# Value products of two units in one block, and square roots moved behind the last split, in a decoder's grouped attention

## What is computed

```
q = (x @ wq.T).reshape(B, N, N_Q, HD).transpose(0, 2, 1, 3)
k = (x @ wk.T).reshape(B, N, N_KV, HD).transpose(0, 2, 1, 3)
v = (x @ wv.T).reshape(B, N, N_KV, HD).transpose(0, 2, 1, 3)
s = jnp.einsum('bhgnd,bhmd->bhgnm', qg, k) * scale
s = jnp.where(mask[None, None, None], s, jnp.asarray(-jnp.inf, s.dtype))
p = jax.nn.softmax(s, axis=-1)
o = jnp.einsum('bhgnm,bhmd->bhgnd', p, v)
return o.reshape(...) @ wo.T
...
x = _layernorm(x + _L1_attn_ref(x, L1_attn_wq, L1_attn_wk, L1_attn_wv, L1_attn_wo), axis=-1)
```

## Time and profile before

| | |
|---|---|
| Median of 3 runs | 1655.85 us (1654.79 to 1658.16) |
| The profiled execution | 1656.58 us, its span 1654.7 us |
| TensorE busy | 1582.0 us, 96% |
| VectorE, ScalarE, GpSimd busy | 59%, 40%, 11% |
| DMA | 75.18 MB, mean 45 GB/s |
| Sublayer D on the trace | from about 835 to 1418 us |
| Sublayer B on the trace | from about 182 to 783 us |

### The profile page before, as it was taken

The page is one execution under the profiler, slowest core; times in us unless marked ns, Lnnn a source line. Parts: engine busy times, 40 slices in busy tenths (PEclk is TensorE's granted clock), DMA queues, the critical chain, the costliest instruction groups (busy, mean ns, idle before and its releaser), DMA issues. The chain is left out here.

```text
span 1654.7 us, 22796 instructions
## 1 busy us (share of the span) xinstructions
PE 1582.0 (96%) x8512; PEld 1270.0 (77%) x8512; DVE 970.2 (59%) x1958; ACT 665.4 (40%) x1218; POOL 178.4 (11%) x134
## 2 busy tenths in 40 slices
PE   7999899999999999998989999999999999889998
PEld 6776777887787778776877788788878877777876
DVE  5998677757765775767424533452553346256655
ACT  4784443434433443434233323332332323346541
POOL 8101400000000000000240000000000000613330
PEclk9999999999999999999999999999999999999999
DMA  5110111101100110100111100110110100202221
GB/s 217 53 40 27 65 36 42 52 1 52 62 16 27 51 44 8 52 26 2 45 53 51 52 26 26 49 52 0 51 63 13 38 14 26 79 10 85 79 83 51
DMA packets 25883, 75.18 MB, mean 45 GB/s; under 512 B 3874, under 2 KB 4610, under 8 KB 25540
## 3 DMA queue, kind: packets, MB, share of 16 engines
q1 hardware_dynamic: 25412, 72.90, 13.1%
q0 software_dynamic: 384, 1.05, 0.2%
HBM read 71.84 MB, written 2.10 MB: 45 GB/s over the span
## 5 line engine op out<-in xcount | busy, mean ns | idle before, releaser
L83 PE MATMUL bankY<-sb_Dwo,sb_DoT 128*128 128x512 f32 x768 | 193.9, 402 | 0.3 <-DVE sb_DoT L1121 0.3
L83 PE MATMUL bankY<-sb_Bwo,sb_BoT 128*128 128x512 f32 x768 | 193.6, 401 | 0.2 <-DVE sb_BoT L1121 0.2
L83 PE MATMUL bankA<-sb_xT,sb_Bwq 128*128 128x512 f32 x768 | 191.6, 399 | 0.0
L83 PE MATMUL bankA<-sb_xT,sb_Dwq 128*128 128x512 f32 x768 | 189.9, 396 | 0.0
L83 PEld LDWEIGHTS bankY<-sb_Dwo,sb_DoT 128*128 128x128 f32 x768 | 141.0, 189 | 42.2 <-issue 13.3
L83 PEld LDWEIGHTS bankY<-sb_Bwo,sb_BoT 128*128 128x128 f32 x768 | 141.0, 189 | 41.9 <-issue 12.9
L83 PEld LDWEIGHTS bankA<-sb_xT,sb_Bwq 128*128 128x128 f32 x768 | 143.4, 190 | 34.3 <-issue 2.7
L83 PEld LDWEIGHTS bankA<-sb_xT,sb_Dwq 128*128 128x128 f32 x768 | 142.2, 188 | 33.9 <-issue 2.7
L1052 DVE TENSOR_TENSOR sb_BqT<-bankA,sb_Btable 128x512 f32<-128x512 f32 x64 | 44.3, 692 | 153.0 <-ACT sb_Bsw L949 153.0
L1088 DVE TENSOR_TENSOR sb_xtok<-sb_xtok,bankY 128x512 f32<-128x512 f32 x128 | 87.1, 681 | 54.6 <-PE bankY L83 54.5
L949 ACT ACTIVATE sb_Bsw<-bankA 64x512 f32<-64x512 f32 x160 | 94.8, 593 | 54.8 <-PE bankA L83 51.6
(11 more groups left out here) (286 smaller groups left out, 2917.8 us busy)
## 6 DMA issues: line engine op xcount, KB each, us to landing
sb_raw<-in_w_attn SPq DMA_DIRECT2D x80, 512.0 KB, 3.4
sb_raw<-in_q_gu SPq DMA_DIRECT2D x22, 256.0 KB, 2.7
sb_raw<-in_q_d SPq DMA_DIRECT2D x11, 256.0 KB, 2.6
sb_raw<-in_wqk SPq DMA_DIRECT2D x8, 256.0 KB, 2.6
sb_rawx<-in_xT SPq DMA_DIRECT2D x4, 512.0 KB, 6.8
sb_raw<-in_ctxT SPq DMA_DIRECT2D x4, 512.0 KB, 6.0
sb_xtok<-in_x_tok SPq DMA_DIRECT2D x1, 2048.0 KB, 12.7
sb_raw<-in_ctx_tok SPq DMA_DIRECT2D x4, 512.0 KB, 3.8
```

The source lines that it names most:

```text
L83: last = nc.tensor.matmul(out, lhs, rhs, start=start and i == 0, stop=stop and i == len(pairs) - 1)
```

## The change

In D (without `rope`) the value products of units u-1 and u are made together in the odd turn u, unit by unit into two halves of `bankO`; one copy and one split of twice the width serve both. Y stands two units behind: turn u makes Y(u-2), between S(u+2) and the value products, and turns 7 and 15 end with Y(u-1), Y(u). From unit 10 of the last pass value products, copies and splits are single again. The exponential of u+2 stands ahead of the copy of `bankO` on ScalarE. Residual adds are three units behind. In B the value products stay single and in their places, though in two halves of `bankO` by turns, and Y stays one behind. In both, the first group's square roots stand behind the copy of unit 15, and the residual add of unit 13 with its statistics stands behind the split of unit 15.

```diff
-            oT = [[sb(mem, f"{tag}oT{i}{p}", [P, GROUP, 2, S], F32R) for p in range(2)] for i in range(2)]
+            oT = [sb(mem, f"{tag}oT{p}", [P, 2, GROUP, 2, S], F32R) for p in range(2)]
...
+            behind = 2 if rope else 3
...
+            def alone(u, final):
+                return rope or (final and u >= 10)
+            def attended(u, last):
+                return (u,) if alone(u, last) else (u - 1, u) if u % 2 else ()
...
+                    def attend(part, u):
+                        units = attended(u, part.final)
+                        if units and u < NT:
+                            pe.wait_ge(v_done, part.it * 4 + u // 2 + 1)
+                        for v in units:
+                            if v == units[0]:
+                                pe.wait_ge(pt_done, part.unit(u) + 3)
+                                pe.wait_ge(o_low, part.unit(v) + 1)
+                            for b in range(2):
+                                rows = slice(S * b, S * b + S)
+                                done = nc.tensor.matmul(bankO[:, b, side(v)], V[rows, v % NT, v // NT * HD:(v // NT + 1) * HD], pt[v % 2][rows, :], start=True, stop=True)
+                            done.then_inc(o_ready, 1)
...
-                            if late(u):
+                            if rope and late(u):
                                 output(part, u - 1)
...
+                            elif not rope and u % NT >= 2:
+                                output(part, u - 2)
+                            attend(part, u)
+                            if rope and u % NT and not late(u):
                                 output(part, u - 1)
...
                             if u % NT == NT - 1:
+                                if not rope:
+                                    output(part, u - 1)
                                 output(part, u)
...
+                            if not rope and not late(u) and (u + 2 < SLOTS or not part.final):
                                 exp(part, u + 2)
+                            units = attended(u, part.final)
+                            if units:
+                                act.wait_ge(o_ready, part.unit(u) + 1)
+                            if len(units) == 1:
+                                nc.scalar.activation(of_unit(0, u), unit_bank(u), ACT.Copy).then_inc(o_high, 1)
+                            elif units:
+                                nc.scalar.activation(of_pair(0), pair_bank, ACT.Copy).then_inc(o_high, 2)
...
+                            if part.final and u == SLOTS - 1:
+                                ln_roots(act, norm + 1, 0)
...
-                            if part.final and u == SLOTS - 2:
-                                ln_roots(act, norm + 1, 0)
...
-                            if u % NT >= 2:
-                                residual(part, u - 2)
+                            if u % NT >= behind and not (rope and part.final and u == SLOTS - 1):
+                                residual(part, u - behind)
...
                             if u % NT == NT - 1:
+                                if not rope or part.final and u == SLOTS - 1:
+                                    residual(part, u - 2)
                                 residual(part, u - 1)
```

More of the change, by code:

```diff
@@ L873, in output @@
                         pe.wait_ge(y_done, part.unit(u) + 1)
-                        pairs = [x for h in range(GROUP) for x in three([o[:, h].rearrange("p b q -> p (b q)") for o in oT[u % 2]], [w[:, h, :] for w in wo])]
+                        pairs = [x for h in range(GROUP) for x in three([o[:, u % 2, h].rearrange("p b q -> p (b q)") for o in oT], [w[:, h, :] for w in wo])]
                         if u % NT == NT - 1:
@@ L900, in turn @@
                                 project(part, banks[0])
-                            if late(u):
+                            if rope and late(u):
                                 output(part, u - 1)
-                            if u < NT and u % 2 == 0:
-                                pe.wait_ge(v_done, part.it * 4 + u // 2 + 1)
-                            pe.wait_ge(pt_done, part.unit(u) + 3)
-                            pe.wait_ge(o_low, part.unit(u) + 1)
-                            for b in range(2):
-                                rows = slice(S * b, S * b + S)
-                                done = nc.tensor.matmul(bankO[:, b, 0:GROUP * S], V[rows, u % NT, u // NT * HD:(u // NT + 1) * HD], pt[u % 2][rows, :], start=True, stop=True)
-                            done.then_inc(o_ready, 1)
-                            if u % NT and not late(u):
+                            elif not rope and u % NT >= 2:
+                                output(part, u - 2)
+                            attend(part, u)
+                            if rope and u % NT and not late(u):
                                 output(part, u - 1)
@@ L1004, in turn @@
                                 queries_or_keys(part, banks[0])
[L1005 to L1008 removed]
+                            if not rope and not late(u) and (u + 2 < SLOTS or not part.final):
                                 exp(part, u + 2)
+                            units = attended(u, part.final)
[5 more added lines that the diff above has]
+                                nc.scalar.activation(of_pair(0), pair_bank, ACT.Copy).then_inc(o_high, 2)
+                            if rope and not late(u) and (u + 2 < SLOTS or not part.final):
+                                exp(part, u + 2)
+                            if part.final and u == SLOTS - 1:
+                                ln_roots(act, norm + 1, 0)
                             if u in VALUES_AT and not part.final:
```

22 lines of the change are left out of this document (15 added, 7 removed).

## The result

| | before | with the change |
|---|---|---|
| first set, median (least to most) | 1656.21 us (1654.79 to 1658.16), 4 runs | 1644.95 us (1642.64 to 1646.71), 4 runs |
| ratio, 95% interval | | 0.9929 [0.9917, 0.9941] |
| second set, median | 1658.81 us, 17 runs | 1642.99 us (1642.41 to 1646.24), 6 runs |
| ratio, 95% interval | | 0.9911 [0.9895, 0.9928] |
| profiled execution: its time, its span | 1656.58, 1654.7 us | 1642.64, 1640.7 us |

The kernel became faster by 0.7 to 0.9%. The forecast was 1640.3 us and its range 1636.5 to 1646.5: the time lies inside, 4.65 us above the forecast in the first set and 2.7 in the second. Against the kernel before of the same set it is 11.3 and 15.8 us less, where the sum said 15.5. The profiled execution, against which the sum was made, came 14.0 us lower.

What follows compares the result with a forecast made beforehand. TensorE, busy 96% of the span, was taken to bound the kernel. 11.9 - 2.1 + 3.3 + 2.4 = 15.5 us off 1655.85 gave 1640.3 us; range 1636.5 to 1646.5.

Steps and rivals of the forecast that it cites:

- Value products by twos: D's loop: two value products in one block cost 1.25 us instead of 1.66; 0.41 saved in 29 pairs, 11.9 us.
- The rival from the Trainium skill: D's pairs: the second unit's weight loads aren't hidden, or a pair drains in part; 6.4 us less gain, 1647; 6%.
- Waits in D's loop: D, turns 1 and 9: TensorE waits 0.25 us for the wider split ahead of Y(0) and Y(8); eight places, -2.1 us.
- The end of D: A(15)'s wait, Y(13)'s wait and the low clock go, 4.1 us; the normalisation takes back 0.8; 3.3 us remain.
- the chain: Normalisation at the block ends: 4.5 us from Y(15) to the next block, where there were 3.7; takes back 0.8.
- The Trainium skill's drain of 1.38 us: Block ends: a drain beside the table load of 1.28 makes the first group 0.7 us later at each, the sum 1.4 smaller.
- The end of B: Load and roots leave A(15)'s wait, 1.6 us; low clock goes, 1.6; the normalisation takes back 0.8; 2.4 us gained.
- with 0.6 of wait left: End of B: 1.6 of A(15)'s 2.21 us wait goes; it still waits 0.6 for its copy behind unit 14's.
- The low clock: Rival: 0.50 clock comes at both block starts, up to 1.6 us lost at each; 1642 to 1643; 25%.
- comes at another place: The clock rival's form: TensorE stands about 2.5 us behind Y(15) and its transposes, bringing low clock at block starts; 25%.

Runs made afterwards that it cites:

- the fourth experiment: Changed kernel with the exponential of unit u+2 behind the output copy again in turns 1 and 9 of D alone; measured 1640.41 us.
- The fifth experiment: Changed kernel with one full-row 128 x 128 transpose of the identity between the two value products of each pair of D; measured 1654.01 us.
- the second experiment: Changed kernel with both ends put back: first group's roots behind unit 14's output copy, unit 13's residual ahead of unit 15's split; 1646.33 us, ratio 0.992.
- the paired B: Changed kernel with B paired in the same way as D, exponential ahead of the copy; measured 1660.92 us, ratio 1.0036.

## Why the prediction was right, and where it was off

**Value products by twos** (11.9 us): right, the saving a little larger. The block takes 1.06 us by waves 0.32, 0.21 and 0.21 apart, as put. A middle pass of D fell by 2.79 and 2.83 us, where 8 x 0.41 - 0.5 = 2.8 was forecast. Part of that agreement is luck: by the passes of the fourth experiment a pair saves 0.43, so 29 x 0.434 = 12.6 us in all as an estimate, and the waits take 2.7. The two misses cancel, 9.9 us for a forecast of 9.8. The fifth experiment measured the price of a change of form by itself at 0.35 us. The rival from the Trainium skill ("TensorE: Matmul & The Clock Gate", Part 3), by which a weight load overlaps running matmuls only where its row group differs, is out: the loads of the second unit run under matmuls of the same row groups, and the pair costs no 0.22 more.

**Waits in D's loop** (2.1 us): right in place and cause, the term too small. The waits stand ahead of Y(0) and Y(8) alone and are 0.34 us each, 2.7 in all, as their removal showed. The split ends 1088.51 - 1082.96 = 5.55 us behind T(9), just as forecast, but the output product starts only 0.10 behind the end of the split, and the sum had no term for that. T(9) came at 3.91 behind T(8) for a forecast of 3.89.

**The end of D** (3.3 us): right in size, for a reason that was half wrong. A(15) waits no more, the 0.50 clock behind it is gone, the chain is 4.61 us for 4.5. My ground for it was loose: I named the moved roots and Y(13) in one breath, and the second experiment shows that Y(13) alone does it. The moved roots and split only lengthened the chain there; without them the end would have given 0.9 us more. The Trainium skill's drain of 1.38 us at a table load ("ScalarE: Activation LUTs", "What ACT_TABLE_LOAD costs") isn't there in this kernel either: load 1394.78 to 1396.06, roots at 1396.07.

**The end of B** (2.4 us): 1.8. The failing step is "with 0.6 of wait left": I followed the copy of the probabilities and not the banks. A(15) also waits for the split of unit 14, which ended at 766.93, so only 1.1 of the 1.6 us came back.

**The low clock** was the rival with 25%, and it came, in the form "comes at another place". It was put at 1642 to 1643. That the profiled execution took 1642.64 is luck, since it holds two amounts that the rival had not priced, 2.17 us lost and 2.1 gained. Its places were half right. Behind D it stood under transposes and a wait for weights and cost nothing. Behind B it cost 1.75 us. The 2.17 ahead of D's projections stand at a wait that the change doesn't touch; and among twelve profiles with the same wait it comes in seven. B's loop gave 2.1 us in the same way: the profile of before has a wait of 1.7 us at 525 and a stretch of 0.50 at 527, that of after a wait of 1.2 and no low clock. The stretch is there in five of the twelve experiments' profiles; others have waits of up to 2.0 us there and stay at 1.00.

So of the miss of 1.5 us in the profile, 3.9 are low clock, 0.5 the split at the end of B, and 3.0 came back ahead of and in B's loop. The median of the first set misses by 3.1 us more, since the profiled execution was the fastest of its four, 2.3 below their median, while that of before lay 0.7 above its own. The range took all this in.

## What to carry to other kernels

Where matmuls in a row-tiled form stand alone between full-size ones, each costs its way in and out, 0.35 to 0.43 us here, where no weight load runs ahead across the change of form; putting two together pays it once. Before moving the copy that releases the next product, look at what stands ahead of it on its engine: an exponential that waits for a third engine cost 0.34 us a place in D and 1.2 of the 2.0 in B, and one condition took that away. When a wait is removed, ask which semaphores the instruction waits for, that for its output bank as well as that for its operand. Price the low clock of TensorE at each remaining wait as a chance, not as a fixed cost: filling those waits with idle transposes made the stretch around them 3.9 us shorter in one pair of profiles, and the times leave it at 0 to 4 us.

## What the runs showed of the hardware

- A weight load that belongs to another form (64 rows, then 128) starts together with its own matmul, 0.33 us after the last load of the form before; within a form it runs under the matmuls of the same row groups.
- A copy (ScalarE) and a subtraction (VectorE) of 1024 elements a row out of two banks took 1.00 and 1.23 us, those of a weight block out of one run 1.06 and 1.22.
- The output product starts 0.10 us behind the end of the split that it waits for (1088.51, 1088.61), and 0.11 in the paired B (393.62, 393.73).
- The same wait of 3.7 us was followed by a granted clock of 0.50 that slowed the next products by 1.9 to 2.3 us in seven profiles, and didn't slow them in five. With transposes in the wait the clock stayed at 1.00 there in both profiles.
